# First attention: two heads stacked on the partitions, three score products of 64 rows

## The chip, the cores and the metric

The kernel runs on one core of one Trainium2 chip. The metric is the device time of one execution in microseconds (us), lower is better; times compared are medians of several runs. The engines are TensorE (PE; its weight loads are listed as PEld), VectorE (DVE), ScalarE (ACT), GpSimd (POOL) and SyncE (SP). Each has its own queue of instructions, and they meet at semaphores only.

## The reference, cut to what matters

Two layers of cross-attention and mixture of experts over x (4 x 1024 tokens of 256), with a context of 4 x 77 rows of 192. The change is in the first attention. Its queries come from x, its keys and values from the context rows and from x itself (1101 keys a batch), with 4 heads of 64:

```python
x = x + _L0_xattn_ref(ctx_768, _layernorm(x, axis=-1), mask_BxS2_bk0, ...)
...
q = ln @ Wq.T
kv = jnp.concatenate([xn @ Wkv.T, ln @ Wlkv.T], axis=1)
...
qn = rmsnorm(q, qn_g) * SCALE
kn = rmsnorm(k, kn_g)
attn = jnp.einsum('bhid,bhjd->bhij', qn, kn)
...
attn = jax.nn.softmax(attn, axis=-1)
out = jnp.einsum('bhij,bhjd->bhid', attn, v)
```

After it come the first experts stage, a second attention over the context alone, and the second experts stage.

## The kernel before, in words

The program is one sequence of stages, each a block in which every engine has its own hand-written order; a block ends when all engines are done. `attention0_inputs` (lines 115 to 302) makes the context's normalised keys `kn`, 77 rows of 16 (batch, head) pairs. `attention0` (line 332 on) runs over 4 batches of 1024 tokens, eight tiles of 128 (`TB`) each.

A number in fp32 is split into a high and a low fp16 part, h and l. Query and key are written as q = qh + ql, k = kh + kl. In `hl` each head has three pieces side by side, h, l, h again (ACT writes pieces 0 and 2 in one copy, line 608, DVE the difference into piece 1, line 723). PE turns them (lines 486 and 489): one transpose puts a head's (h, l) of 2 x 64 on 128 partitions. The queries take 4 transposes a tile, the keys 8: "form" 0 as (h, l), form 1 as (l, h). A score is then two matmuls over 128 rows: form 0 gives kh.qh + kl.ql, form 1 gives kl.qh + kh.ql.

**Tile part.** `pipeline` staggers the stages of eight tiles (`LAG` 4). Tile by tile: DVE centres (696), PE turns (462), ACT scales (591), PE projects q, k and v (473, 475), ACT squares and copies v (600, 601), DVE sums (702, 705), POOL takes the power -0.5 (674), DVE normalises (712, 716), ACT and DVE split (608, 723), PE turns the parts (486, 489), ACT copies the keys (613) and DVE the queries (727) out of PSUM. `turn_parts` of a tile waits until both copies of the tile before are done. Of every second tile, ACT and DVE also split a piece of the experts' weights (619, 752), which SP loads and stores. The first two tiles' transposes and projections of the next batch are issued at the end of the batch before.

**Loop.** 36 steps a batch (`STEPS`): 4 units (half of the queries, pair of heads) of 9 key tiles, the ninth being the 77 context rows (`kctx`). PE's order for every even n is: scores of n+1, scores of n+2, values of n, values of n+1. Scores of a step are 4 matmuls of 512 query columns (line 507), two for each of the pair's two heads; head j goes to its own PSUM bank `sc[:, n % 2, j]`. ACT makes exp of both heads in one instruction (647), DVE adds it up for the denominators (667, 663), and PE multiplies it with v in fp32, the two heads side by side on 64 columns each (518). An fp32 matmul shows as two records. Scores of step n+1 wait for the exp of step n-1 (they share banks); exp of step n waits for the sum of step n-4 (4 buffers `probs`). Behind each unit come the denominators (527), DVE's reciprocal and product (732, 736), and behind each half the output projection (540) with DVE's residual (744). ACT and DVE split one more weight piece in every unit.

POOL begins each batch with two small copies (683, 684) behind the first projection, and counts them in `vc_done`, for which PE and ACT wait before they use the context rows:

```python
pool.wait_ge(mm_done, b * TB + 1)
pool.tensor_copy(cshift[:], g.shift[0:M, bass.ds(b, 1)]).then_inc(vc_done, 1)
pool.tensor_copy(v[0:M, TB, :], g.vctx[:, bass.ds(b, 1), :].rearrange("p o d -> p (o d)")).then_inc(vc_done, 1)
```

Of the kernel before, what the change touches and what calls it, by code (L numbers as in the profile page):

```python
# [17 lines left out]
F16 = mybir.dt.float16  # L18
# [7 lines left out]
P = 128  # L26
# [86 lines left out]
def attention0_inputs(nc, g, a):  # L113


    with ExitStack() as st:
# [15 lines left out]
        khl = m.sb("khl_c", [M, B * H0, 3, HD0], F16)  # L132
# [33 lines left out]
        def _(act):  # L166
# [3 lines left out]
            for v, dst in ((a["ln_x_g"], gx), (a["ln_x_b"], bx)):  # L170
# [21 lines left out]
            act.copy(khl[:, :, 0:3:2, :], kn[:].rearrange("p (h o) d -> p h o d", o=1).to_broadcast([M, B * H0, 2, HD0])  # L192
                     ).then_inc(hi_done, 1)
            act.wait_ge(kt_done, 1)
            t16 = tr[:].bitcast(F16)
            for n in range(4):
                act.copy(g.kctx[:, n // 2, (n % 2) * 8:(n % 2) * 8 + 8, 0:M],
                         t16[:, n, 0:8 * MP].rearrange("p (h m) -> p h m", h=8)[:, :, 0:M]).then_inc(kt_ev, 1)
            act.wait_ge(kt_ev, 4)
# [22 lines left out]
        def _(dve):  # L222
# [48 lines left out]
            dve.tensor_tensor(khl[:, :, 1, :], kn[:], khl[:, :, 0, :], ALU.subtract).then_inc(v_step, 1)  # L271
# [3 lines left out]
        def _(pe):  # L275
# [22 lines left out]
            for n in range(2):  # L298
                for h in range(B * H0):
                    last = pe.transpose(t16[:, 2 * n + h // 8, (h % 8) * MP:(h % 8) * MP + M],  # L300
                                        khl[:, h, n:n + 2, :].rearrange("p o d -> p (o d)"), g.ident16[0:M, 0:M])
# [30 lines left out]
def attention0(nc, g, a):  # L332
# [7 lines left out]
    with ExitStack() as st:  # L340
# [8 lines left out]
        hl = m.sb("hl0", [P, 2, 2 * H0, 3, HD0], F16)  # L349
        qT = m.sb("qT", [P, H0, S], F16)  # L350
        kT = m.sb("kT", [P, 2, H0, S], F16)
# [15 lines left out]
        t3 = hi[:].bitcast(F16).rearrange("p a (h t) -> p a h t", t=P)  # L367
# [86 lines left out]
        def _(pe):  # L454
# [23 lines left out]
            def turn_parts(first, l):  # L478
# [6 lines left out]
                for h in range(H0):  # L485
                    pe.transpose(t3[:, 0, h, :], hl[:, i, h, 0:2, :].rearrange("p o d -> p (o d)"), g.ident16[:])
                for form in range(2):
                    for h in range(H0):
                        last = pe.transpose(t3[:, 1, form * H0 + h, :],
                                            hl[:, i, H0 + h, form:form + 2, :].rearrange("p o d -> p (o d)"), g.ident16[:])  # L490
                last.then_inc(t3_done, 1)

            def scores(b, n, fresh):
                u, k = divmod(n, KT)
                half, pair = divmod(u, 2)
                if not fresh:
                    pe.wait_ge(e_done, STEPS * b + n - 1)
                for j in range(2):
                    h = 2 * pair + j
                    q = qT[:, h, half * HALF:(half + 1) * HALF]  # L500
                    for form in range(2):
                        if k < TB:
                            kk = kT[:, form, h, k * P:(k + 1) * P]
                        else:
                            kk = g.kctx[:, form, bass.ds(b * H0 + h, 1), 0:M]
                            kk = kk.rearrange("p o m -> p (o m)")
                        last = pe.matmul(sc[0:rows(k), n % 2, j, :], kk, q, start=(form == 0), stop=(form == 1))  # L507
                last.then_inc(s_done, 1)
# [35 lines left out]
            def body(b, more):  # L544
# [6 lines left out]
                pe.wait_ge(vc_done, 2 * b + 2)  # L551
# [31 lines left out]
        def _(act):  # L583
# [19 lines left out]
            def high(first, l):  # L603
                t, i = first + l, l % 2
                act.wait_ge(n_done, t + 1)
                if l >= 2:
                    act.wait_ge(t3_done, t - 1)
                act.copy(hl[:, i, :, 0:3:2, :],
                         qk[:, i].rearrange("p (h o) d -> p h o d", o=1).to_broadcast([P, 2 * H0, 2, HD0])).then_inc(hi_done, 1)

            def keys_out(first, l):
                act.wait_ge(t3_done, first + l + 1)
                act.copy(kT[:, :, :, l * P:(l + 1) * P], t3[:, 1].rearrange("p (f h) t -> p f h t", f=2)  # L613
                         ).then_inc(e3_act, 1)
# [12 lines left out]
            def body(b, more):  # L627
# [4 lines left out]
                for n in range(STEPS):  # L632
# [11 lines left out]
                    if n == TB:  # L644
                        act.wait_ge(vc_done, 2 * b + 2)
# [1257 lines left out]
```

## Time and profile before

| | us |
|---|---|
| median of 3 runs | 1844.99 |
| lowest and highest | 1844.53, 1845.87 |
| the profiled execution | 1844.98 |
| its span in the profile | 1843.3 |
| mean granted TensorE clock | 0.922 of full |
| PE busy | 1593.0 (86%) |
| DVE, ACT, POOL busy | 1115.1, 853.1, 705.1 |
| first attention: tile part and loop of batch 1 | 58.6 to 93.2, 93.2 to 170.0 |
| of batch 4 | 445.3 to 481.1, 481.1 to 558.4 |

The span is what the profiler covers; the execution's own time is 1.7 us longer. "Idle <- releaser" in a row is how long the engine had nothing to do ahead of it, and whose instruction ended that. PE's matmul records overlap: a record lasts until its result is out, so what a matmul costs in a stream is the distance from its start to the next one's. Shapes stand as rows*columns of the weights, then the moving operand.

### The profile page before, as it was taken

What the parts mean: (1) busy time and instruction counts of PE and PEld (TensorE: products, weight loads), DVE (VectorE), ACT (ScalarE), POOL (GpSimd) and SP (SyncE); (2) the same over time, 40 slices, a digit from 0 to 9 for tenths busy, and PEclk for the clock granted to TensorE, in tenths of its full rate; (3) what the DMA queues carried; (4) which work ended last, traced back from release to release, by engine and by line L of the source; (5) the groups of instructions that cost most, each with busy time, mean ns of one, the idle gap of its engine ahead of it and who ended that gap; (6) DMA issues with size and microseconds to landing.
All of it is one profiled execution on the core that took longest, in us unless ns stands there. A gap on an engine that the chain in (4) does not pass through costs nothing. (4 is left out here: it accounts for less than half of the span.)

```text
span 1843.3 us, 38924 instructions
## 1 busy us (share of the span) xinstructions
PE 1593.0 (86%) x12460; PEld 1169.2 (63%) x12461; DVE 1115.1 (60%) x1945; ACT 853.1 (46%) x1518; POOL 705.1 (38%) x517
## 2 busy tenths in 40 slices
PE   4799798898897669999999996799988689999997
PEld 1433434434336658888888883577767568888886
DVE  4677687677687844555554441788876834444443
ACT  1664764755653425555554441376664322222221
POOL 2400401202200015555555442477771046555564
PEclk9999899899896589999999997699996789999999
DMA  4321311320414554555553222300005353333333
GB/s 132 100 79 46 114 55 36 114 68 23 138 35 168 187 206 92 137 137 137 137 137 69 46 41 38 92 25 17 8 24 180 106 149 59 59 62 60 57 60 44
DMA packets 104311, 159.85 MB, mean 87 GB/s; under 512 B 10810, under 2 KB 69998, under 8 KB 104110
## 3 DMA queue, kind: packets, MB, share of 16 engines
q1 hardware_dynamic: 73007, 117.52, 19.6%
q0 software_dynamic: 29952, 40.91, 12.6%
q8 instruction: 43, 0.70, 0.2%
q10 hardware_dynamic: 1279, 0.46, 0.1%
q14 instruction: 30, 0.25, 0.0%
HBM read 91.49 MB, written 67.37 MB: 86 GB/s over the span
## 5 line engine op out<-in xcount | busy, mean ns | idle before, releaser
L1249 PE MATMUL e_ph<-e_zTt,weights_a 128*128 128x256 f16 x3744 | 425.4, 274 | 29.3 <-issue 27.2
L1249 PEld LDWEIGHTS e_ph<-e_zTt,weights_a 128*128 x3744 | 360.9, 98 | 93.5 <-issue 49.8
L1203 POOL DMA_INDIRECT e_zt<-token_parts,slot_token x156 | 163.6, 1049 | 209.2 <-issue 198.4
L1382 DVE TENSOR_TENSOR e_hl<-e_h,e_hh 128x512 f16<-128x512 f32 x156 | 104.5, 691 | 228.4 <-ACT e_hh L1348 228.4
L1334 ACT ACTIVATE e_h<-e_ph,e_b 128x256 f32<-128x256 f32 x312 | 130.6, 470 | 232.8 <-PE e_ph L1249 155.8
L1213 POOL DMA_INDIRECT token_rows<-e_ysb,slot_token x78 | 148.2, 1901 | 206.9 <-DVE e_ysb L1399 192.5
L1263 PE MATMUL e_pyt<-weights_b,e_hh 128*128 x1248 | 210.7, 273 | 0.7 <-DVE e_ysb L1399 0.7
L647 ACT ACTIVATE probs<-lower_banks,shift 128x1024 f32<-128x1024 f32 x128 | 137.6, 1110 | 119.4 <-PE lower_banks L507 114.4
L1213 POOL DMA_INDIRECT out_dram<-e_ysb,slot_token x78 | 124.4, 1595 | 131.4 <-DVE e_ysb L1403 107.8
L1263 PE MATMUL e_pyt<-weights_b,e_hl 128*128 x624 | 170.2, 273 | 0.0
L1373 DVE SCALAR_TENSOR_TENSOR e_g<-e_ph,e_h 128x512 f32<-128x512 f32 x78 | 54.0, 692 | 174.1 <-PE e_ph L1249 174.1
L667 DVE TENSOR_TENSOR acc<-acc,probs 128x1024 f32<-128x1024 f32 (+1 forms) x112 | 136.9, 1222 | 28.7 <-ACT probs L647 25.5
L518 PE MATMUL middle_banks<-probs,v 128*64 128x512 f32 (+1 forms) x576 | 142.6, 606 | 1.0 <-ACT probs L647 1.0
L507 PE MATMUL lower_banks<-qT,kT 128*128 128x512 f16 x512 | 131.6, 402 | 4.6 <-ACT kT L613 4.6
L1263 PEld LDWEIGHTS e_pyt<-weights_b,e_hh 128*128 128x128 f16 x1248 | 122.1, 98 | 14.7 <-issue 1.0
L1337 ACT ACTIVATE e_h<-e_ph 128x512 f32<-128x512 f32 x78 | 46.6, 597 | 169.6 <-PE e_ph L1249 169.6
L507 PEld LDWEIGHTS lower_banks<-qT,kT 128*128 128x128 f16 x512 | 46.8, 101 | 106.0 <-issue 33.1
L1263 PE MATMUL e_pyt<-weights,e_hh 128*128 x624 | 108.6, 273 | 0.5 <-DVE e_ysb L1403 0.5
L683 POOL COPY cshift<-shift 77x1 f32 x4 | 0.7, 183 | 279.5 <-PE middle_banks L475 279.5
L1715 POOL TENSOR_TENSOR s<-s,rs 128x1232 f32<-128x1232 f32 x32 | 72.7, 2273 | 51.7 <-DVE rs L1783 51.6
L1348 ACT CAST e_hh<-e_h 128x512 f16<-128x512 f32 x156 | 92.3, 619 | 0.0
L1348 ACT CAST e_hh<-e_g 128x512 f16<-128x512 f32 x78 | 48.2, 618 | 83.5 <-DVE e_g L1373 83.5
(231 smaller groups left out, 2952.5 us busy)
## 6 DMA issues: line engine op xcount, KB each, us to landing
weight_parts<-w_split SPq DMA_DIRECT2D x32, 512.0 KB, 3.3
weights_a<-weight_parts SPq DMA_DIRECT2D x16, 1024.0 KB, 7.4
x_sb<-in_u SPq DMA_DIRECT2D x24, 512.0 KB, 5.1
weight_parts<-x_sb SPq DMA_DIRECT2D x24, 512.0 KB, 3.4
w_raw<-in_w1T SPq DMA_DIRECT2D x16, 512.0 KB, 4.4
w_raw<-in_w2T SPq DMA_DIRECT2D x16, 512.0 KB, 4.7
weights_b<-weight_parts SPq DMA_DIRECT2D x8, 1024.0 KB, 9.6
token_parts<-x_sb SPq DMA_DIRECT2D x8, 1024.0 KB, 5.3
```

The source lines that it names most:

```text
L507: last = pe.matmul(sc[0:rows(k), n % 2, j, :], kk, q, start=(form == 0), stop=(form == 1))
L518: last = pe.matmul(po[u % 2][j * HD0:(j + 1) * HD0, :], v[0:rows(k), k, h * HD0:(h + 1) * HD0], pr[0:rows(k), n % 4, j, :], start=(k == 0) ...
L647: act.activation(pr[0:r, n % 4], sc[0:r, n % 2], ACT.Exp, bias=bias).then_inc(e_done, 1)
L667: dve.tensor_tensor(acc[0:r, u % 2], acc[0:r, u % 2], pr[0:r, n % 4], ALU.add).then_inc(acc_done, 1)
L1203: pool.indirect_dma_start(zt[:, i % 2, c, :], None, g.zrows, at).then_inc(ld[i % 2], 16)
L1213: pool.indirect_dma_start(g.rows[layer], at, ysb[:, s, c, :], None, compute_op=ALU.add).then_inc(sto[s], 16)
L1249: last = pe.matmul(ph[:, q, f, :], up_w(wp, e, k, 2 * q + f), zTs[:, s, 2 * zp + k, :], start=(n == 0), stop=(n == 5))
L1263: last = pe.matmul(py[c][:, 0, :], hp[:, s, f, c * P:(c + 1) * P], down_w(wp, e, f), start=(n == 0), stop=(n == 3 * NF - 1))
L1334: last = act.activation(h32[:, q % 2, f, :], ph[:, q, f, :], ACT.Relu, bias=b1[:, bass.ds(e, 1), 2 * q + f], scale=1.0 / WS)
L1348: act.copy(hh[:, s, 2 * q:2 * q + 2, :], src[:, q % 2]).then_inc(hi_done, 1)
L1382: dve.tensor_tensor(hl[:, s, 2 * q:2 * q + 2, :], src[:, q % 2], hh[:, s, 2 * q:2 * q + 2, :], ALU.subtract).then_inc(lo_done, 1)
L1715: pool.tensor_tensor(s[:, i], s[:, i], per_key(rs[:, i, :]), ALU.mult).then_inc(n_done, 1)
```

## The change

Query and key parts are now laid out as high parts of all heads, then low parts of all heads (`hl[:, i, part, head]`), with no third piece. One transpose takes the same part of two neighbouring heads, so that the pair's heads stand on partitions 0 to 63 and 64 to 127; a tile takes 4 transposes for the queries and 4 for the keys. `qT` and `kT` have the indices part and pair. A score is three products of 64 rows: kh.qh, kh.ql, kl.qh (kl.ql is left out), and the six matmuls of a step go head 0, head 1, head 0, head 1 and so on. The context keys are laid out in the same way (16 transposes instead of 32, two copies instead of four), and POOL copies a batch's context keys behind its 1024 keys in `kT`, so that all steps read `kT`; `vc_done` counts three a batch.

```diff
@@ -129,7 +129,7 @@
         kn = m.sb("kn_c", [M, B * H0, HD0])
-        khl = m.sb("khl_c", [M, B * H0, 3, HD0], F16)
+        khl = m.sb("khl_c", [M, 2, B * H0, HD0], F16)
         mask = m.sb("mask_c", [M, B], U8)
@@ -189,14 +189,13 @@
             act.wait_ge(v_step, 16)
-            act.copy(khl[:, :, 0:3:2, :], kn[:].rearrange("p (h o) d -> p h o d", o=1).to_broadcast([M, B * H0, 2, HD0])
-                     ).then_inc(hi_done, 1)
+            act.copy(khl[:, 0], kn[:]).then_inc(hi_done, 1)
             act.wait_ge(kt_done, 1)
             t16 = tr[:].bitcast(F16)
-            for n in range(4):
-                act.copy(g.kctx[:, n // 2, (n % 2) * 8:(n % 2) * 8 + 8, 0:M],
-                         t16[:, n, 0:8 * MP].rearrange("p (h m) -> p h m", h=8)[:, :, 0:M]).then_inc(kt_ev, 1)
-            act.wait_ge(kt_ev, 4)
+            for n in range(2):
+                act.copy(g.kctx[:, n, :, 0:M],
+                         t16[:, n, 0:2 * B * MP].rearrange("p (h m) -> p h m", m=MP)[:, :, 0:M]).then_inc(kt_ev, 1)
+            act.wait_ge(kt_ev, 2)
 
@@ -268,7 +267,7 @@
             dve.wait_ge(hi_done, 1)
-            dve.tensor_tensor(khl[:, :, 1, :], kn[:], khl[:, :, 0, :], ALU.subtract).then_inc(v_step, 1)
+            dve.tensor_tensor(khl[:, 1], kn[:], khl[:, 0], ALU.subtract).then_inc(v_step, 1)
             dve.wait_ge(v_step, 22)
@@ -296,9 +295,9 @@
             for n in range(2):
-                for h in range(B * H0):
-                    last = pe.transpose(t16[:, 2 * n + h // 8, (h % 8) * MP:(h % 8) * MP + M],
-                                        khl[:, h, n:n + 2, :].rearrange("p o d -> p (o d)"), g.ident16[0:M, 0:M])
+                for h in range(2 * B):
+                    last = pe.transpose(t16[:, n, h * MP:h * MP + M],
+                                        khl[:, n, 2 * h:2 * h + 2, :].rearrange("p o d -> p (o d)"), g.ident16[0:M, 0:M])
             last.then_inc(kt_done, 1)
@@ -346,9 +345,9 @@
         qk = m.sb("qk0", [P, 2, 2 * H0, HD0])
-        hl = m.sb("hl0", [P, 2, 2 * H0, 3, HD0], F16)
-        qT = m.sb("qT", [P, H0, S], F16)
-        kT = m.sb("kT", [P, 2, H0, S], F16)
+        hl = m.sb("hl0", [P, 2, 2, 2 * H0, HD0], F16)
+        qT = m.sb("qT", [P, 2, 2, S], F16)
+        kT = m.sb("kT", [P, 2, 2, S + MP], F16)
         v = m.sb("v0", [P, KT, D])
@@ -364,7 +363,7 @@
         pv = [mid[:, i, 0:D] for i in range(2)]
-        t3 = hi[:].bitcast(F16).rearrange("p a (h t) -> p a h t", t=P)
+        t3 = hi[:].bitcast(F16).rearrange("p a (h t) -> p a h t", t=P)[:, :, 0:4, :].rearrange("p a (f n) t -> p a f n t", f=2)
         sc = lo[:].rearrange("p (s j) q -> p s j q", s=2)
@@ -482,12 +481,12 @@
                     pe.wait_ge(e3_dve, t)
-                for h in range(H0):
-                    pe.transpose(t3[:, 0, h, :], hl[:, i, h, 0:2, :].rearrange("p o d -> p (o d)"), g.ident16[:])
-                for form in range(2):
-                    for h in range(H0):
-                        last = pe.transpose(t3[:, 1, form * H0 + h, :],
-                                            hl[:, i, H0 + h, form:form + 2, :].rearrange("p o d -> p (o d)"), g.ident16[:])
+                for what in range(2):
+                    for part in range(2):
+                        for pair in range(2):
+                            h = what * H0 + 2 * pair
+                            last = pe.transpose(t3[:, what, part, pair, :],
+                                                hl[:, i, part, h:h + 2, :].rearrange("p o d -> p (o d)"), g.ident16[:])
                 last.then_inc(t3_done, 1)
@@ -495,16 +494,12 @@
                     pe.wait_ge(e_done, STEPS * b + n - 1)
-                for j in range(2):
-                    h = 2 * pair + j
-                    q = qT[:, h, half * HALF:(half + 1) * HALF]
-                    for form in range(2):
-                        if k < TB:
-                            kk = kT[:, form, h, k * P:(k + 1) * P]
-                        else:
-                            kk = g.kctx[:, form, bass.ds(b * H0 + h, 1), 0:M]
-                            kk = kk.rearrange("p o m -> p (o m)")
-                        last = pe.matmul(sc[0:rows(k), n % 2, j, :], kk, q, start=(form == 0), stop=(form == 1))
+                for product, (kp, qp) in enumerate(((0, 0), (0, 1), (1, 0))):
+                    for j in range(2):
+                        dims = slice(j * HD0, (j + 1) * HD0)
+                        last = pe.matmul(sc[0:rows(k), n % 2, j, :], kT[dims, kp, pair, k * P:k * P + rows(k)],
+                                         qT[dims, qp, pair, half * HALF:(half + 1) * HALF],
+                                         start=(product == 0), stop=(product == 2))
                 last.then_inc(s_done, 1)
@@ -548,7 +543,7 @@
                 pe.wait_ge(e3_dve, first + TB)
-                pe.wait_ge(vc_done, 2 * b + 2)
+                pe.wait_ge(vc_done, 3 * b + 3)
                 scores(b, 0, True)
@@ -605,13 +600,11 @@
                     act.wait_ge(t3_done, t - 1)
-                act.copy(hl[:, i, :, 0:3:2, :],
-                         qk[:, i].rearrange("p (h o) d -> p h o d", o=1).to_broadcast([P, 2 * H0, 2, HD0])).then_inc(hi_done, 1)
+                act.copy(hl[:, i, 0], qk[:, i]).then_inc(hi_done, 1)
 
 ...
                 act.wait_ge(t3_done, first + l + 1)
-                act.copy(kT[:, :, :, l * P:(l + 1) * P], t3[:, 1].rearrange("p (f h) t -> p f h t", f=2)
-                         ).then_inc(e3_act, 1)
+                act.copy(kT[:, :, :, l * P:(l + 1) * P], t3[:, 1]).then_inc(e3_act, 1)
 
@@ -642,7 +635,7 @@
                     if n == TB:
-                        act.wait_ge(vc_done, 2 * b + 2)
+                        act.wait_ge(vc_done, 3 * b + 3)
                     bias = g.shift[:, B:B + 1] if k < TB else cshift[:]
@@ -681,6 +674,7 @@
                 pool.tensor_copy(cshift[:], g.shift[0:M, bass.ds(b, 1)]).then_inc(vc_done, 1)
+                pool.tensor_copy(kT[:, :, :, S:S + M], g.kctx[:, :, bass.ds(2 * b, 2), 0:M]).then_inc(vc_done, 1)
                 pool.tensor_copy(v[0:M, TB, :], g.vctx[:, bass.ds(b, 1), :].rearrange("p o d -> p (o d)")).then_inc(vc_done, 1)
@@ -720,11 +714,11 @@
                 dve.wait_ge(hi_done, t + 1)
-                dve.tensor_tensor(hl[:, i, :, 1, :], qk[:, i], hl[:, i, :, 0, :], ALU.subtract).then_inc(lo_done, 1)
+                dve.tensor_tensor(hl[:, i, 1], qk[:, i], hl[:, i, 0], ALU.subtract).then_inc(lo_done, 1)
 
 ...
                 dve.wait_ge(t3_done, first + l + 1)
-                dve.tensor_copy(qT[:, :, l * P:(l + 1) * P], t3[:, 0, 0:H0, :]).then_inc(e3_dve, 1)
+                dve.tensor_copy(qT[:, :, :, l * P:(l + 1) * P], t3[:, 0]).then_inc(e3_dve, 1)
 
@@ -1846,7 +1840,7 @@
             m = Mem(nc, st)
-            g.kctx = m.sb("kctx", [P, 2, B * H0, MP], F16)
+            g.kctx = m.sb("kctx", [P, 2, 2 * B, MP], F16)
             g.vctx = m.sb("vctx", [M, B, D])
```

## Rows read from the trace of the kernel before

**Rows 1.** Busy time by stretch (93.2:170.0, 221.7:299.1, 351.6:429.0, 481.1:558.4), the four loops

```profile
core 0: us, PE busy (x) PEld busy (x) DVE busy (x) ACT busy (x) POOL busy (x), PEclk, DMA share, GB/s
...
sum 308.90, PE 303.69 PEld 102.69 DVE 234.14 ACT 171.82 POOL 4.17; mean PE 75.92 PEld 25.67 DVE 58.54 ACT 42.95 POOL 1.04
```

**Rows 2.** The same view, the four tile parts (58.6, 187.0, 315.6, 445.3 on)

```profile
sum 141.10, PE 103.99 PEld 66.96 DVE 107.34 ACT 108.13 POOL 67.15; mean PE 26.00 PEld 16.74 DVE 26.83 ACT 27.03 POOL 16.79
```

**Rows 3.** The page, part 2: granted TensorE clock in 40 slices of 46 us

```profile
PEclk9999899899896589999999997699996789999999
```

**Rows 4.** Timeline, second batch's loop: start, us, engine line op out<-in xcount [idle <-releaser]

```profile
248.16 1.90 PE L507 MATMUL lower_banks<-qT,kT 128*128 128x512 f16 x8
249.33 1.11 ACT L647 ACTIVATE probs<-lower_banks,shift 128x1024 f32<-128x1024 f32 x1 [2.46 <-PE lower_banks L507]
249.99 1.94 PE L518 MATMUL middle_banks<-probs,v 128*64 128x512 f32 x8
250.35 1.05 ACT L619 ACTIVATE w_split<-w_raw 128x1024 f16<-128x1024 f32 x1
...
251.29 1.10 ACT L647 ACTIVATE probs<-lower_banks,shift 128x1024 f32<-128x1024 f32 x1
...
251.86 1.90 PE L507 MATMUL lower_banks<-qT,kT 128*128 128x512 f16 x8
```

**Rows 5.** Groups of the page: line engine op out<-in xcount | busy us, mean ns | idle

```profile
L507 PE MATMUL lower_banks<-qT,kT 128*128 128x512 f16 x512 | 131.6, 402 | 4.6 <-ACT kT L613 4.6
```

**Rows 6.** Timeline of PE, one tile of the second attention, and a projection of the first

```profile
1206.66 0.81 PE L1652 MATMUL psc<-kcur,qT 32*128 32x154 f32 x16
...
208.43 1.03 PE L475 MATMUL middle_banks<-wqkv,lnT 128*128 128x256 f32 x4
```

**Rows 7.** Timeline, half 0's output and the end of the second batch's loop

```profile
276.29 0.69 DVE L744 TENSOR_TENSOR x_sb<-x_sb,upper_banks 128x512 f32 x1 [1.05 <-PE upper_banks L540]
277.03 1.99 PE L540 MATMUL upper_banks<-wo,oT 128*128 128x256 f32 x8 [0.96 <-DVE x_sb L744]
...
287.49 3.36 DVE L732 RECIPROCAL rden<-upper_banks 128x512 f32<-128x512 f32 x1 [0.18 <-PE upper_banks L527]
...
291.49 4.99 DVE L667 TENSOR_TENSOR acc<-acc,probs 128x1024 f32<-128x1024 f32 x4
...
297.53 2.47 DVE L667 TENSOR_TENSOR acc<-acc,probs 128x1024 f32<-128x1024 f32 x2
...
300.38 0.44 PE L462 MATMUL lower_banks<-ident,z 128*128 128x128 f32 x2 [1.34 <-DVE z L696]
```

**Rows 8.** Timeline, two tiles of the second batch's tile part

```profile
197.67 1.03 ACT L613 COPY kT<-upper_banks 128x1024 f16<-128x1024 f16 x1
...
199.68 1.23 DVE L752 SCALAR_TENSOR_TENSOR w_split<-w_raw,w_split 128x1024 f16<-128x1024 f32 x1 [0.48 <-ACT w_split L619]
```

**Rows 9.** Groups of the page, an ACT cast of 512 elements in the experts stage

```profile
L1348 ACT CAST e_hh<-e_h 128x512 f16<-128x512 f32 x156 | 92.3, 619 | 0.0
```

**Rows 10.** Timeline, end of the second tile part and the first scores

```profile
209.52 0.61 PE L489 MATMUL upper_banks<-ident,hl 128*128 128x128 f16 x8
...
219.48 1.06 PE L489 MATMUL upper_banks<-ident,hl 128*128 128x128 f16 x8
220.58 1.01 ACT L613 COPY kT<-upper_banks 128x1024 f16<-128x1024 f16 x1 [1.85 <-PE upper_banks L489]
...
221.72 5.28 PE L507 MATMUL lower_banks<-qT,kT 128*128 128x512 f16 x12 [1.18 <-ACT kT L613]
```

**Rows 11.** Timeline, the context stage

```profile
38.17 6.50 POOL L329 TENSOR_TENSOR rstd<-stat_ve,neghalf 128x32 f32<-128x32 f32 x1 [3.58 <-DVE stat_ve L323]
...
39.25 1.90 ACT L192 CAST khl_c<-kn_c 77x2048 f16<-77x2048 f32 x1 [8.19 <-DVE kn_c L254]
...
42.55 2.24 PE L300 MATMUL tr_c<-ident,khl_c 77*128 77x77 f16 x32 [13.44 <-DVE khl_c L271]
...
44.82 2.40 ACT L197 COPY kctx<-tr_c 128x616 f16<-128x616 f16 x4 [3.67 <-PE tr_c L300]
```

**Rows 12.** Groups of the page, POOL's first copy of a batch

```profile
L683 POOL COPY cshift<-shift 77x1 f32 x4 | 0.7, 183 | 279.5 <-PE middle_banks L475 279.5
```

## The prediction

> **What bounds the kernel now.** I read the 40 slices first, then the busy time by stage, the waits and groups of TensorE (PE), and last the timeline of one stage. The change touches the first attention and the short context stage ahead of it alone, so the question is what sets the pace there. The rest follows it in a chain and should move as a whole.
>
> The first attention has four batches, each with two parts. In the **loop** (36 steps: scores, exp, values) PE is busy 303.7 us of 308.9, VectorE (DVE) 234, ScalarE (ACT) 172 [rows 1]. So PE sets the pace, with DVE at 76%. In the **tile part** (eight tiles: projection, norm, split, transposes; 141.1 us in the four) PE is busy 104, DVE 107, ACT 108, about three quarters each [rows 2]. There no engine is the bound: they wait for one another in turn. The PEclk line is at 9 tenths in this stretch (slices 2 to 12), but at 8 in the fifth, eighth and eleventh, where a tile part ends [rows 3]: PE runs at its lower level, 1.2 GHz, for a while there.
>
> Inside the loop, a pair of steps is eight score matmuls, then eight value records. The scores start at 248.16 and last 1.90 us, the values start at 249.99, the next scores at 251.86 [rows 4]: a period of 3.70 us for two steps. Eight score matmuls in 1.90 us, the last taking 0.38 from its start, are one per (1.90 - 0.38) / 7 = 0.217 us, near enough to the 0.213 of 512 columns at 2.4 GHz. The score group is 512 such matmuls, 131.6 us busy [rows 5], and 64 more over the context keys.
>
> **Scores, three products for four.** Before: 4 matmuls of 128 rows a step. After: 6 of 64 rows, alternately on partitions 0-63 and 64-127, into different banks. What six cost hangs on whether the two halves of the array run side by side. The trace has no 64-row pair, but it has a 32-row group: L1652 puts 16 records of 154 columns, four row groups in turn, into 0.81 us [rows 6]. Their neighbour of 256 columns runs 4 records in 1.03 us, (1.03 - 0.38) / 3 = 0.215 each [rows 6], so 154 columns should take 0.13, and 16 in series 2.1 us. They took 0.81: row groups do run side by side. Bounds for one pair of matmuls: 0.217 us (perfect overlap) to 0.434 (none). I take 0.217, as the 32-row row is much nearer to overlap. A step is then 3 x 0.217 = 0.65 instead of 0.87, a gain of 0.217 (with exact streaming, 0.214) a step, 7.7 us a batch, **30.9 us** over 144 steps, if nothing else ends last.
>
> The Trainium skill, page "TensorE: Matmul & The Clock Gate", section "Measured speedup vs the span model", gives 3.07x for four row tiles of 512 columns, and also a model in which tiles cost some 4 ns each. By the model the gain is the 30.9; by 3.07 of 4, applied to two, a pair would cost 1.3 matmuls and three pairs nearly as much as four matmuls do now. The rows settle less than I would like; this is a rival below.
>
> **What takes some of it back in the loop.**
> - ACT's extra weight cast of 1.05 us, once in 9 steps, sits between two exps (249.33 and 251.29), and the second ends at 252.39 [rows 4]. The second half of the scores from 251.86 waits for it; it starts at 252.72 now. After the change it would want to start 0.64 earlier (three pair slots saved), at 252.08, while the exps are only 0.21 earlier, at 252.18: 0.1 to 0.2 us with the semaphore, four times a batch: 0.8 at most.
> - For an ordinary pair of steps: the first exp starts 1.17 us after its scores and could start 0.21 earlier, so it ends 1.17 - 0.21 + 1.11 = 2.07 after the scores begin. The values that need it are the second half of the group from 249.99, some 0.9 behind that time: 2.7 after the scores begin, then 2.3 [rows 4]. The slack shrinks from 0.4 to 0.2: no stall.
> - DVE in 9 steps: 8 sums of 1.25 (four take 4.99), 4.00 from the reciprocal's start to the next sum, one weight split of 1.25: 15.3 us [rows 7, 8]. PE's nine steps are 9 x 1.85 and about 0.9 for the denominators (half a value group), 17.5, and become 15.6. It fits on average, not locally. After the reciprocal at 287.49, DVE runs without a break through 291.49 + 4.99 and the last sums at 297.53 + 2.47 = 300.0, and PE's first transpose of the next batch waits 1.34 us for it at 300.38 [rows 7]. So the batch's last 12.5 us are DVE's already: the 5 steps of scores that PE does behind 287.49 give nothing, 5 x 0.214 = 1.07 us lost a batch.
> - The output of the first half waits 0.96 us between its two halves for DVE's residual, which now starts as soon as PE is done (DVE idle 1.05 before it) [rows 7]. PE arrives 1.3 us earlier, DVE does not: I put 0.7 us a batch on it.
>
> Loop in all: 7.7 - 0.8 - 1.1 - 0.7 = 5.1 a batch, **20.6 us**. Bounds: 30.9 (all hidden) and about 12 (twice these losses and more at the start of a unit).
>
> **Tile part.** ACT's split copy and key copy go from 1024 written elements to 512: 1.03 us for the key copy now [rows 8], 0.62 for an ACT cast of 512 elsewhere [rows 9], so about -0.42 each. DVE's subtraction and query copy keep their 512 elements. Transposes go from 12 to 8: 8 in 0.61 at full and 1.06 at half clock, so 0.056 or 0.107 each [rows 8, 10], -0.22 or -0.43.
> - Middle: in a tile with a weight piece DVE waits 0.48 for ACT's weight cast, which is behind the key copy [rows 8]. That goes; then comes DVE's own order, norm to sums to POOL's power to norm, which the change leaves. Two such tiles a batch: -1.0.
> - Tail: the last tiles wait on one another. The last transposes end at 220.54, the key copy follows, the scores start at 221.72 after it [rows 10]. Fewer transposes -0.43, key copy -0.43, and the weight cast behind the previous key copy, which holds up DVE, moves by both, of which I count 0.75: -1.6.
> Together -2.6 a batch, **-10.2 us**; bounds 0 below (if DVE and POOL alone set the pace) and 16 above.
>
> The first 12 score matmuls of a batch take 5.28 us, 0.427 each: half clock [rows 10]. Three slots of it cost 1.3 less, but the clock then comes back later in the work; I count them at 0.214 like the rest, and leave ±1 us a batch.
>
> **Context stage.** The chain: cast of 2048 elements 1.90 us, 32 transposes 2.24, four copies 2.40, ending 47.22; POOL's power ends at 44.67 [rows 11]. After: cast about 1.0 (half the elements), 16 transposes -1.0, two copies -1.2, together -3.1; but POOL's 44.67 becomes the last. **-2.5 us**; bounds 0 to 3.1.
>
> **POOL's new copy** of context keys (308 elements) joins two copies, the first of 0.18 us, which start after 279.5 us of idle time in four goes [rows 12]; behind it is only the power of the next tile. It is hidden under the projection and squares; without that cover, under 1 us a batch. PE and ACT wait for one more vc_done, long in. SP's queue is not touched.
>
> **Sum.** 20.6 + 10.2 + 2.5 = 33.3 off. The profiled run took 1844.98 us (span 1843.3), the median is 1844.99, so no correction: **1811.7 us**.
>
> **Rivals.**
> 1. Row groups overlap poorly. L1652's 16 records are four rounds, three gaps in 0.81 - 0.29 = 0.52, 0.17 each, where 154 columns need 0.13: 1.3 times. If that isn't just the first round after a switch, three pairs cost 3 x 0.28 = 0.85, as now. Only the 12.7 outside the loop stays: 1832. For: the arithmetic. Against: the scores' own first gap behind the values is hardly longer than the others (eight in 1.90 us leave no room for it) [rows 4], and that a first round is long after a change of layout explains the rest. Chance 0.1. The skill's 3.07x (same page) would give the same 1832.
> 2. DVE becomes the bound of the whole loop. Then units run at 15.3 plus gaps in DVE from waits for exp, and the loop gains 10 to 12: 1844.98 - 12.7 - 11 = 1821. For: no-idle DVE in the last unit. Against: 234 of 309 busy. The skill's "TensorEngine Tiling (Array Packing)", section "PSUM Bottleneck", says just this: a faster array leaves the evacuation as it was. Chance 0.15.
> 3. **Slower**: the two 64-row groups don't overlap with 128 weight columns each, so six matmuls take 6 x 0.214. Place: the score line; price 2 x 0.214 x 144 = 61.8, less 12.7: +49, 1894. It decides as soon as a pair costs over 1.5 matmuls. Against: L1652 has 128 weight columns too, in fp32, and overlaps [rows 6]. Chance 0.08.
> 4. All hidden, clock returns early: -30.9 - 12.7 - 2: 1799. Chance 0.12.
>
> **Chances.** Forecast 0.55, rivals as above. The range 1798 to 1828 takes in the forecast, rivals 2 and 4 and the bounds of the loop's losses; it leaves out 1 and 3 and the forecast's own tails. A measurement here can tell about 0.2% (3.7 us) from no change. Faster by more 0.89; within 0.03, the worst of rival 1, where the tile part gives nothing either; slower 0.08, rival 3.
>
> **What would show it.** The score line: 864 records, starting in pairs a few ns apart, pairs 0.214 apart; busy some 100 to 110 us, with the context keys' (before, 131.6 for the 512 alone). If single records stand 0.214 apart, rival 3. The loop near 72 us a batch instead of 77.2 (308.9 / 4), with more waits of PE for exp and DVE; if DVE is over 90% busy there, rival 2. The tile part near 32.7 us a batch from 35.3 (141.1 / 4), with the DVE wait on the weight cast gone. The key and split copies at 0.6 us. The first z at 45.2. If the copies are short and the tile part as long as before, POOL and DVE were its bound and step "tile part" is wrong.

## Result, and the profile after

The changed kernel takes 1812.56 us (median of 4 runs, 1811.81 to 1814.75), the kernel before 1845.24 (4 runs): a ratio of 0.9825, 95% interval [0.9808, 0.9842], or 32.7 us less. Forecast were 1811.7 us, 33.5 less than the 1845.2 measured here, and a range of 1798 to 1828. The number came out within 1 us; not all parts of the sum did.

The two profiled executions, 1843.3 and 1810.7 us in span, cut at the same points of the work:

| stretch | before | after | difference | forecast |
|---|---|---|---|---|
| context stage, up to the first z | 47.7 | 44.9 | -2.8 | -2.5 |
| tile parts, from the first split copy to the first scores | 141.1 | 128.9 | -12.2 | -10.2 |
| loops, from the first scores to the last values | 308.9 | 278.9 | -30.0 | -30.9, less 10.3 |
| from a loop's last values to the next tile part, or to the stage's end | 63.7 | 71.3 | +7.6 | part of the 10.3 |
| everything behind the first attention | | | +4.8 | 0 |

The groups of the changed kernel's page, which answer to [rows 5] and [rows 12] (line engine op out<-in xcount | busy us, mean ns | idle before):

```profile
L500 PE MATMUL lower_banks<-qT,kT 64*128 64x512 f16 (+1 forms) x864 | 114.5, 397 | 2.9 <-ACT kT L607 2.9
...
L676 POOL COPY cshift<-shift 77x1 f32 x4 | 0.7, 183 | 255.7 <-PE middle_banks L474 255.7
```

864 records are busy 114.5 us, somewhat more than the 100 to 110 forecast; of the kernel before, the 512 over x's keys alone were busy 131.6. The loops take 69.7 us a batch (278.9 / 4), where about 72 was forecast: part of the loss that I had put into the loop came behind it.

Busy time by stretch, changed kernel: the four loops, the four tile parts, then the four stretches behind the loops (columns as in [rows 1]):

```profile
core 0: us, PE busy (x) PEld busy (x) DVE busy (x) ACT busy (x) POOL busy (x), PEclk, DMA share, GB/s
...
sum 278.90, PE 272.12 PEld 86.42 DVE 229.24 ACT 171.67 POOL 4.17; mean PE 68.03 PEld 21.61 DVE 57.31 ACT 42.92 POOL 1.04
...
sum 128.90, PE 92.56 PEld 56.52 DVE 104.00 ACT 81.78 POOL 67.28; mean PE 23.14 PEld 14.13 DVE 26.00 ACT 20.45 POOL 16.82
...
sum 71.30, PE 47.77 PEld 27.96 DVE 45.30 ACT 12.14 POOL 9.84; mean PE 11.94 PEld 6.99 DVE 11.32 ACT 3.04 POOL 2.46
```

PE is still busy 98% of the loops; DVE has come up from 76% to 82%. The timeline of a unit (start, us, what) answers to [rows 4]:

```profile
232.45 1.47 PE L500 MATMUL lower_banks<-qT,kT 64*128 64x512 f16 x12
233.41 1.11 ACT L640 ACTIVATE probs<-lower_banks,shift 128x1024 f32<-128x1024 f32 x1 [2.02 <-PE lower_banks L500]
233.85 1.94 PE L513 MATMUL middle_banks<-probs,v 128*64 128x512 f32 x8
234.42 1.05 ACT L612 ACTIVATE w_split<-w_raw 128x1024 f16<-128x1024 f32 x1
...
235.37 1.10 ACT L640 ACTIVATE probs<-lower_banks,shift 128x1024 f32<-128x1024 f32 x1
...
235.72 1.63 PE L500 MATMUL lower_banks<-qT,kT 64*128 64x512 f16 x12
```

Twelve matmuls in 1.47 us where eight took 1.90: six slots instead of eight. The period of two steps is 3.27 us (232.45 to 235.72) instead of 3.70. The second group takes 1.63, 0.16 more: that is the wait for the exp behind ACT's weight cast, forecast at 0.1 to 0.2. In each batch two pairs of steps are longer in this way, by 0.06 to 0.16, not four.

Behind the loop, changed kernel, the same places as [rows 7]:

```profile
258.84 1.99 PE L535 MATMUL upper_banks<-wo,oT 128*128 128x256 f32 x8 [1.33 <-DVE x_sb L738]
...
268.43 3.36 DVE L726 RECIPROCAL rden<-upper_banks 128x512 f32<-128x512 f32 x1
...
278.47 2.47 DVE L660 TENSOR_TENSOR acc<-acc,probs 128x1024 f32<-128x1024 f32 x2
...
281.32 0.44 PE L461 MATMUL lower_banks<-ident,z 128*128 128x128 f32 x2 [2.25 <-DVE z L690]
```

From the reciprocal to the last sum's end DVE needs 12.5 us as before (268.43 to 280.94, then 287.49 to 300.00). PE gets through its last scores faster and waits 2.25 us for z instead of 1.34; the output waits 1.33 instead of 0.96.

The tile part (answers to [rows 8] and [rows 10]):

```profile
187.85 0.60 ACT L607 COPY kT<-upper_banks 128x512 f16<-128x512 f16 x1
...
189.44 1.23 DVE L746 SCALAR_TENSOR_TENSOR w_split<-w_raw,w_split 128x1024 f16<-128x1024 f32 x1 [0.15 <-ACT w_split L612]
...
205.17 1.01 PE L488 MATMUL upper_banks<-ident,hl 128*128 128x128 f16 x8 [2.31 <-DVE qT L721]
...
207.24 1.01 PE L488 MATMUL upper_banks<-ident,hl 128*128 128x128 f16 x8 [1.06 <-DVE qT L721]
208.28 0.59 ACT L607 COPY kT<-upper_banks 128x512 f16<-128x512 f16 x1 [1.48 <-PE upper_banks L488]
...
209.00 4.13 PE L500 MATMUL lower_banks<-qT,kT 64*128 64x512 f16 x18 [0.75 <-ACT kT L607]
```

The key copy is 0.60 instead of 1.03, DVE's wait for the weight cast 0.15 instead of 0.48, and the last groups of transposes follow each other 2.07 us apart (205.17 to 207.24) instead of 2.86 (216.62 to 219.48). The scores start at half clock as before, 18 of them in 4.13 us.

### The profile page after: what moved, and what is told of

Its sections match the earlier page's. It is cut to its first block and busy times, and to the rows that moved or that the text cites. A ratio compares the mean times of both kernels' runs of the same rounds, so it can differ in the third digit from the quotient of the medians.

```text
span 1810.7 us, 39194 instructions
## 1 busy us (share of the span) xinstructions
PE 1554.4 (86%) x12604; PEld 1143.3 (63%) x12605; DVE 1110.4 (61%) x1945; ACT 824.6 (46%) x1516; POOL 706.7 (39%) x521
## 5 line engine op out<-in xcount | busy, mean ns | idle before, releaser
L500 PE MATMUL lower_banks<-qT,kT 64*128 64x512 f16 (+1 forms) x864 | 114.5, 397 | 2.9 <-ACT kT L607 2.9
L500 PEld LDWEIGHTS lower_banks<-qT,kT 64*128 64x128 f16 (+1 forms) x864 | 37.4, 99 | 99.9 <-ACT probs L640 41.9
L1612 PE MATMUL pt<-ident,s 128*77 128x128 f32 x512 | 73.8, 290 | 14.6 <-ACT pT L1675 7.0
```

Source lines behind the costliest of these rows:

```text
L500: last = pe.matmul(sc[0:rows(k), n % 2, j, :], kT[dims, kp, pair, k * P:k * P + rows(k)], qT[dims, qp, pair, half * HALF:(half + 1) * HALF ...
L1612: last = pe.transpose(pt[:, n % 2, h % 4, :], s[:, d % SLOT, h, :], g.ident[:])
```

## Experiments

Each kernel ran with the kernel before on the same chip; times are medians of 4 runs, and single runs for the two second traces. The kernel before gave 1846.2 in the first two groups of runs and 1847.1 in the third.

**The order of the six matmuls.**

```diff
-                for product, (kp, qp) in enumerate(((0, 0), (0, 1), (1, 0))):
-                    for j in range(2):
+                for j in range(2):
+                    for product, (kp, qp) in enumerate(((0, 0), (0, 1), (1, 0))):
```

> The changed kernel with the same six 64-row matmuls a step, but head 0's three first, then head 1's three. Theory A (neighbours in different row groups run side by side, and that is the whole gain of the loop): now only head 0's last runs beside head 1's first, and across two steps head 1's last beside head 0's first; 9 slots of 0.214 us for two steps instead of 6, so +1.5 x 0.214 x 144 = +46 us, 1859 us. Rival B (a 64-row matmul is cheaper by itself, whatever its neighbour): no change, 1812 to 1814 us.

Measured: 1815.2 us (0.9835 of before, [0.9819, 0.9852]), 2.6 more than the changed kernel, whose own runs spread over 2.9. Neither 1859 nor a clean proof of B. The timeline of PE:

```profile
243.53 1.48 PE L500 MATMUL lower_banks<-qT,kT 64*128 64x512 f16 x12
```

Twelve in 1.48 us as in turns. In the records the starts still come in pairs, some 9 ns apart where the changed kernel has 3. The records don't name the partitions, so which two ran side by side is an inference: if matmuls on the same rows can't overlap (the next run), head 1's first, queued fourth, ran beside head 0's first. PE then doesn't need neighbours of different row groups, and the part "in turns" of the change does nothing that can be told here. Whether the pair ran abreast at all needed a kernel that can't do it:

**All six on one row group.**

```diff
-                        dims = slice(j * HD0, (j + 1) * HD0)
+                        dims = slice(0, HD0)
```

> The changed kernel with all six matmuls of a step on partitions 0 to 63 (the second head's scores are made from the first head's data; the work is the same in number and size). e1_no_turns has shown that the order of the six does not matter. Theory A (two row groups run side by side, in whatever order they are queued): here nothing can, six slots instead of three, +3 x 0.214 x 144 = +92, less what the slower loop gives back by DVE being on time, about 8: 1897 us. Theory B (a 64-row matmul is cheaper by itself): 1813 us.

Head 1's scores are then made of head 0's data, so this kernel's output is not the attention's; it serves for the time alone. Measured: 1910.7 us, ratio 1.0338 [1.0321, 1.0356]; 98 us above the changed kernel. Timeline of PE, the four loops, and the four stretches behind them:

```profile
261.82 2.32 PE L500 MATMUL lower_banks<-qT,kT 64*128 64x512 f16 x10
...
265.94 2.76 PE L500 MATMUL lower_banks<-qT,kT 64*128 64x512 f16 x12
```

```profile
sum 386.70, PE 381.88 PEld 131.90 DVE 237.90 ACT 177.89 POOL 4.17; mean PE 95.47 PEld 32.97 DVE 59.48 ACT 44.47 POOL 1.04
```

```profile
sum 61.50, PE 43.13 PEld 27.00 DVE 38.50 ACT 12.24 POOL 9.84; mean PE 10.78 PEld 6.75 DVE 9.62 ACT 3.06 POOL 2.46
```

Twelve take 2.76 us, (2.76 - 0.38) / 11 = 0.216 each: a 64-row matmul costs as much as one of 128 rows, and the whole gain of the loop is two row groups side by side. Theory B is out. This is also what rival 3 would have cost: 1911, not the prediction's 1894, nor the 1897 expected here. DVE's slack did come back: the stretches behind the loops are 61.5 us, 9.8 less than in the changed kernel, where I had credited 8. What was too low is the price of the loops, 107.8 us more instead of 92. An ordinary pair of steps takes 4.56 us against 3.27, which makes 93 of it over the 72 pairs of the four batches; the rest lies at the loops' half-rate starts (the first 18 score matmuls of the second batch last 7.86 us against 4.13). The stages behind the attention took 3.3 us more as well.

**A fourth product, and only two.**

```diff
-                for product, (kp, qp) in enumerate(((0, 0), (0, 1), (1, 0))):
+                for product, (kp, qp) in enumerate(((0, 0), (0, 1), (1, 0), (1, 1))):
...
-                                         start=(product == 0), stop=(product == 2))
+                                         start=(product == 0), stop=(product == 3))
```

> The changed kernel with the fourth product kl.ql put back: eight 64-row matmuls a step in turns. It keeps the new layout, transposes and copies. Theory A: four slots a step, the loop is as long as in the kernel before, and only what the tile part and the context stage gave is left: +6.3 us a batch, about 1838 us; each product is worth a slot of 0.214 us, less what DVE took back. Rival B (the gain of the loop came from elsewhere, as from the fewer weight columns read or the copies): 1813 to 1820 us.

> The changed kernel with kh.ql left out as well: two products, four matmuls, two slots a step. If PE still sets the loop alone, it gains another 0.214 x 144 = 30.9 us: 1782 us. If DVE, with 15.3 us of work in 9 steps against 15.6 of PE's now and 13.7 then, is the next bound, the loop gains only some 2 to 3 us a batch: about 1802 us, with DVE over 85% busy in the loop. I expect the second.

Measured: 1835.8 us with four (0.9944, [0.9927, 0.996]), 1802.0 with two (0.9767, [0.9744, 0.979]). The four loops of each:

```profile
sum 307.50, PE 302.56 PEld 102.45 DVE 233.98 ACT 171.61 POOL 4.17; mean PE 75.64 PEld 25.61 DVE 58.49 ACT 42.90 POOL 1.04
```

```profile
sum 266.30, PE 247.21 PEld 68.59 DVE 225.48 ACT 170.10 POOL 5.18; mean PE 61.80 PEld 17.15 DVE 56.37 ACT 42.53 POOL 1.30
```

With four products the loops last 307.5 us, as in the kernel before (308.9). So the layout gives the loop nothing and the third slot everything: 307.5 to 278.9 is 28.6 us, 0.199 a step. The next slot gives 12.6 us, not 28.6: PE's share falls from 98 to 93%, and its longest wait in the loop is now for DVE's residual (waits of PE, second batch's loop; this wait was 1.3 us with three products):

```profile
PE upper_banks L535 <- DVE x_sb L738: 3.3, 1, 3.3
PE lower_banks L500 <- ACT probs L640: 1.0, 3, 0.4
```

DVE's lateness is the next limit that shows, and close, though DVE itself is busy 85% of these loops, not over 90. The four runs spread from 1799.6 to 1807.7 us; the time is the 1802 forecast. Whether DVE alone sets the pace of this loop wasn't tried.

The Trainium skill says that tiling makes PE faster and leaves the evacuation of PSUM as it was ("TensorEngine Tiling (Array Packing)", section "PSUM Bottleneck"). At three slots no run here shows such a limit. At two, the residual that PE waits for does read PSUM, but most of DVE's work in the loop, the sums over `probs`, reads SBUF, so these runs don't show that the evacuation is what held it up.

**The reciprocal on ACT.** This takes 3.4 us a unit away from DVE. The cut shows the main lines; ACT's call for a batch's last unit stands at the head of the next batch, or behind the last loop:

```diff
+            def invert(b, u):
+                act.wait_ge(den_done, UNITS * b + u + 1)
+                if u > 0:
+                    act.wait_ge(o_done, UNITS * b + u)
+                act.activation(rden[:], pden, ACT.Ln).then_inc(ln_done, 1)
+                act.wait_ge(ln_done, UNITS * b + u + 1)
+                act.activation(rden[:], rden[:], ACT.Exp, scale=-1.0).then_inc(r_done, 1)
...
+                    if n in (KT + 4, 2 * KT + 3, 3 * KT + 4):
+                        invert(b, n // KT - 1)
...
-                dve.wait_ge(den_done, UNITS * b + u + 1)
-                dve.reciprocal(rden[:], pden).then_inc(r_done, 1)
```

> The changed kernel with the reciprocal of the denominators (3.36 us on DVE) made on ACT as exp(-ln(x)), two instructions of about 0.6 us. Theory C (DVE's lateness at the end of a batch is what took back part of the gain: PE waits 2.25 us for the next batch's z, and the last output waits for the reciprocal): about 2.2 + 2 us a batch go, 1796 us. Rival (DVE's lateness is covered by PE's and POOL's own chain): under 4 us, 1809 to 1813 us. If the two ACT instructions hold up exp in the loop, slower by 0.5 us a unit, +8 us.

> The kernel before the change, with the reciprocal on ACT as exp(-ln(x)), as in e4_rden_on_act. Theory C (DVE's lateness took back part of the change's gain): the kernel before gains less from this, 1.3 us of waiting for z and 2 us of the last output's chain a batch, 13 us: 1832 us; the change then brings 38 to 39 us (1832 to 1793) instead of 33. Rival (the two are independent): 1845.2 - 19.4 = 1826 us.

Measured: 1793.2 us on the changed kernel (ratio to the kernel before 0.9719, [0.9703, 0.9736]), the fastest version here; on the kernel before 1832.1 (0.9923, [0.9906, 0.9939]). With both on ACT the change brings 38.9 us (1832.1 to 1793.2) instead of 32.7, the 38 to 39 of theory C; the rival's 1826 is out. The four loops of the first, and the four stretches behind them:

```profile
sum 277.90, PE 272.99 PEld 86.19 DVE 196.80 ACT 186.04 POOL 4.17; mean PE 68.25 PEld 21.55 DVE 49.20 ACT 46.51 POOL 1.04
```

```profile
157.70:172.20 14.50, 11.55 (x45) 7.29 (x46) 7.27 (x17) 5.19 (x13) 3.25 (x5) 1.00 0.16 49
...
505.00:516.00 11.00, 6.38 (x20) 4.28 (x20) 3.83 (x9) 1.23 (x2) 0.00 (x0) 0.84 0.08 29
```

The loops are as long as before (277.9), so in them DVE's 32 us less (229.2 to 196.8) change next to nothing. Most of the gain comes behind them: the four stretches take 54.2 us instead of 71.3, which is 17.1 of the 23.0 us between the two traces (19.4 between the medians); 14.5 instead of 18.7 from the last values of the first batch to the next tile part, 11.0 instead of 16.3 at the end. PE waits 0.7 us for z (2.25 in the changed kernel), and the clock stays at full rate there (PEclk 1.00 in the first row; 0.91 in the changed kernel, below). The traced execution is the fastest of its four (1789.5 us; the slowest took 1795.9), and another 4.1 us of its lead over the changed kernel's trace lie in the stages behind the attention (1271.7 instead of 1275.9). So the 38.9 isn't DVE's lateness alone: between the traces of the two kernels with the reciprocal on ACT, the change gives back under 1 us behind the loops, where it was 7.6, but also only 0.4 in the stages behind, where it was 4.8.

**The tile part.** Four more transposes a tile, then ACT's copies at 1024 elements on top:

```diff
+                for part in range(2):
+                    for pair in range(2):
+                        pe.transpose(t3x[:, 1, part, pair, :],
+                                     hl[:, i, part, 2 * pair:2 * pair + 2, :].rearrange("p o d -> p (o d)"), g.ident16[:])
```

```diff
-                act.copy(hl[:, i, 0], qk[:, i]).then_inc(hi_done, 1)
+                act.copy(hl[:, i, 0:3:2], qk[:, i].rearrange("p (o h) d -> p o h d", o=1).to_broadcast([P, 2, 2 * H0, HD0])).then_inc(hi_done, 1)
...
-                act.copy(kT[:, :, :, l * P:(l + 1) * P], t3[:, 1]).then_inc(e3_act, 1)
+                act.copy(kT8[:, :, l * P:(l + 1) * P], hi[:].bitcast(F16).rearrange("p a (h t) -> p a h t", t=P)[:, 1]).then_inc(e3_act, 1)
```

> The changed kernel with four more transposes a tile (12 as before), into PSUM columns that nothing reads. The prediction's tail has the last transposes and, through the weight cast, those of a tile before on the path, 0.43 us each at half clock; the middle tiles cost nothing, since DVE and POOL set the pace. So +0.4 to +0.9 us a batch: 1814.5 to 1816 us. Rival (PE sets the pace of the tile part): 0.22 to 0.43 us in each of 32 tiles, +9 us, 1821 us.

> As e5_twelve_turns, and ACT's two copies of a tile write 1024 elements again, as in the kernel before (the second half goes to places that nothing reads). The tile part should then be as before: by the prediction +2.6 us a batch, 10.2 in all, 1823 us, most of it from the copies. Rival (the tile part was bound by DVE and POOL, and its shortening came from the clock's phase or from the new layout of DVE's writes): under +4 us, 1816 us.

Measured: 1819.0 us with the transposes (0.9851, [0.9835, 0.9868]) and 1825.7 with both (0.9888, [0.9872, 0.9905]): +6.4 and +13.2. The four tile parts of each:

```profile
sum 132.90, PE 102.67 PEld 65.92 DVE 104.31 ACT 82.00 POOL 67.32; mean PE 25.67 PEld 16.48 DVE 26.08 ACT 20.50 POOL 16.83
```

```profile
sum 139.30, PE 101.63 PEld 66.13 DVE 107.18 ACT 108.25 POOL 67.70; mean PE 25.41 PEld 16.53 DVE 26.80 ACT 27.06 POOL 16.93
```

In the tile parts themselves the transposes cost 4.0 us (128.9 to 132.9) and the copies 6.4 more, and the sum of 10.4 is the forecast's 10.2. The 1.0 a batch for the transposes is above my 0.4 to 0.9, but part of it is the clock. A tile part of the changed kernel has two lengths: 31.8 to 32.1 us (PEclk 0.89 to 0.91), or 33.2 (0.87), the latter in the second batch of its first trace and in the third of its second. With the four transposes the batches take 32.7, 33.9, 33.8 and 32.5: 0.7 more than 32.0, 33.2 and 31.8 in the first, second and fourth, and in the third 0.6, set beside the longer kind. Like set beside like, the transposes cost 0.7 a batch, as forecast.

Neither theory's total fits, 1816 or 1821 with the transposes: 2.4 and 2.8 us of the two fell outside the tile parts, where the two kernels do the same as the changed one. In the traces, 1.9 of the first lies in the stages behind the attention; of the second, 1.1 lies ahead of the first tile part, whose start moves by 0.8 between the changed kernel's own two traces. The reason isn't shown.

**What was given back behind the attention.** The stage behind starts 37.4 us earlier (572.3 to 534.9), the end comes 32.6 earlier. The missing 4.8 us can be chance, other in each execution, or come back with the kernel. Both kernels were traced again, one execution each:

> The changed kernel as it is, for a second trace. In the first one the first attention ended 37.4 us earlier than in the kernel before, but the whole only 32.6. [...] Rival (what was given back is a cost of the change): the same 4 to 5 us are given back again, at the same places.

> The kernel before as it is, for a second trace. [...] Rival: the two traces run alike to 0.3 us everywhere.

Measured: 1814.8 and 1848.7 us. In the second pair the stage behind starts 37.6 us earlier and the end comes 33.9 earlier, so 3.7 us are given back. The stages behind took 1271.0 and 1273.1 us in the two traces of the kernel before, 1275.9 and 1276.8 in those of the changed one: a kernel differs from itself by 0.9 or 2.1 us, and from the other by 2.8 to 5.8.

Two places make up most of it. The first is 20 us of the first experts stage, at the same point of the work: the kernel before, its second trace, the changed kernel, its second trace:

```profile
690.00:710.00 20.00, 19.55 (x186) 17.24 (x187) 7.13 (x15) 10.82 (x24) 10.89 (x8) 1.00 0.33 54
```

```profile
691.60:711.60 20.00, 19.55 (x186) 17.33 (x187) 7.18 (x15) 10.76 (x24) 10.89 (x8) 1.00 0.33 54
```

```profile
652.60:672.60 20.00, 19.19 (x167) 16.20 (x168) 6.97 (x15) 9.69 (x21) 9.85 (x8) 0.91 0.28 41
```

```profile
654.30:674.30 20.00, 19.11 (x166) 16.27 (x167) 6.90 (x15) 9.62 (x21) 10.46 (x8) 0.91 0.28 41
```

The changed kernel has a piece of 1.2 GHz there, PEclk 0.91, where the kernel before has 1.00, and gets 167 matmuls done instead of 186. It is one group of 48 that takes 7.08 us instead of 5.41 (timelines of PE, the kernel before, then the changed one):

```profile
689.92 5.41 PE L1249 MATMUL e_ph<-e_zTt,weights_a 128*128 128x256 f16 x48 [1.79 <-issue]
```

```profile
653.00 7.08 PE L1243 MATMUL e_ph<-e_zTt,weights_a 128*128 128x256 f16 x48 [2.08 <-issue]
```

The second place, ahead of the second attention, is no matter of the clock, which is at half rate there in all four traces (PEclk 0.50). DVE waits longer for a load of x (timelines of DVE, the kernel before, then the changed one):

```profile
1157.19 0.43 DVE L1749 BATCH_NORM_STATS2 stats<-x_sb 128x6 f32<-128x256 f32 x1 [2.46 <-DMA x_sb<-token_rows]
```

```profile
1123.77 0.43 DVE L1743 BATCH_NORM_STATS2 stats<-x_sb 128x6 f32<-128x256 f32 x1 [4.09 <-DMA x_sb<-token_rows]
```

In the second traces it waits 2.54 and 3.92 us. PE's next work waits for the z that DVE makes of it, 9.40 us instead of 7.77. A last 1.1 us is lost at the start of the second experts stage in the first pair; in the second pair that loss is made up again.

So both large pieces came back in both traces of a kernel, which makes pure chance unlikely. They aren't a price of the new layout either: the kernel with the reciprocal on ACT has it and took 1271.7 us behind the attention in its trace, its counterpart without the change 1271.3, and the kernels with twelve transposes have it and wait 2.5 us for the load. The kernel with four products and the one on a single row group lose there too (1277.4 and 1279.2 us). It is work that the change doesn't touch. What decides where the half-rate pieces fall and how long the load takes wasn't tried and stays open.

## Why the prediction was right, point by point

- **Bound and main term: right.** PE set the loops' pace, and a pair of 64-row matmuls costs one slot (rows of the fp32 group with 32 rows carried this over [rows 6]). Forecast 30.9 us in the loops before losses; 28.6 between the kernels with four and three products. Rival 1, poor overlap, is out; so is the reading of the Trainium skill's 3.07x for four tiles as 1.5x for two ("TensorE: Matmul & The Clock Gate", "Measured speedup vs the span model"). That section's other model, a few ns for each tile, agrees: 12 records in 1.47 us, in pairs that start some 3 ns apart.
- **What is taken back: the size roughly right, the place not.** The forecast had 10.3 us, all counted in the loops. Measured are 8.5: 0.9 in the loops (30.9 less 30.0) and 7.6 in the stretches behind them. I put 1.1 us a batch on DVE's lateness at the end and 0.7 on the output. Measured in the second batch: 0.91 more waiting for z, and 0.37 more at the output, so that term was twice too large. I put up to 0.8 a batch on ACT's weight cast: it is at most 0.16 for each of two groups, 0.3. A part I hadn't listed is the clock. The stretch from the second batch's last values to the next tile part runs partly at 1.2 GHz, as the row of the changed kernel shows beside the one before:

```profile
279.10:297.20 18.10, 13.45 (x45) 7.77 (x46) 12.14 (x19) 4.07 (x11) 3.25 (x5) 0.91 0.17 58
```

```profile
299.10:315.60 16.50, 11.77 (x45) 7.28 (x46) 11.20 (x18) 4.04 (x10) 2.85 (x4) 1.00 0.18 57
```

  The same 45 matmuls are busy 13.45 us instead of 11.77, and that is the whole difference of 1.6 between the two stretches. The changed kernel has 0.91 there in all three batches that have a next one; the kernel before has 0.90 in its first batch and 1.00 in two; with the reciprocal on ACT, where PE waits only 0.7 us for z, it is 1.00 in all three. In the first batch, where both kernels ran partly at the lower level, the 1.7 us lost are idle time of PE. That the longer wait brings the clock down fits these rows; it wasn't tried by itself.
- **Tile part: right.** 12.2 us measured, 10.2 forecast; some of the 12.2 is the clock, as two tile parts of the kernel before were of a longer kind (36.0 and 35.8 us against 34.6 and 34.7) and one of the changed kernel. Like set beside like it is 2.6 to 2.8 a batch, some 11 in all. The copies cost 6.4 us when widened again and the transposes 0.7 a batch. Of DVE's wait for the weight cast 0.15 us is left, where I had written that it goes.
- **The prediction's own sums** hold to 0.2 us: 4 x 5.1 is 20.4, not 20.6, and 4 x 2.6 is 10.4, not 10.2, which cancel.
- **Context stage: right.** z starts 2.8 us earlier, 0.3 of it from a load; POOL's power, not the keys, is now the last.
- **POOL's copy: right.** It takes 0.44 us, in idle time.
- **The step that was missing** is what happens behind the attention. I wrote that the rest "should move as a whole". It gave back 4.8 us, and 3.7 in the second pair of traces. Without that the change would have brought 37.4 us where I forecast 33.3: the losses were 1.8 smaller, the tile part 2.0 and the context stage 0.3 larger. That the total came out within 1 us is luck, a gain forecast too low against a loss that I hadn't seen.
- **Rival 2** (DVE bounds the loop): not at three products, since taking 32 us from DVE left the loops at 277.9. At two products PE waits for DVE, but DVE is busy 85%, below the 90 that I had named as the sign.
- **Rival 3** (no overlap) was priced too low: forced, it gives 1911 us, not 1894.

## What to carry to other kernels

A contraction over 64 rows that is stacked up to 128 to fill the array can be taken apart again: two matmuls on different halves of the partitions, into different banks, cost one slot here (12 in 1.47 us), so three products of two heads cost three slots, not four. Before taking more from the bound engine, look at who finishes last at the end of a loop: here a 3.36 us reciprocal on DVE was worth 19 us on the changed kernel and 14 on the one before, with next to no effect inside the loop (1.0 us). And split an expected gain at the stage's end as well as at the kernel's: in stages that weren't touched, one group of matmuls met a half-rate piece of the clock (1.7 us) and one load took longer (1.6 us).

## What was not expected of the hardware

- The order of matmuls on two row groups didn't matter: three for rows 0 to 63 queued ahead of three for rows 64 to 127 took 1.48 us for two steps, against 1.47 in turns. By strict order of the queue, nine slots would have been needed for two steps, and a slot of one row group costs 0.216; so matmuls of different row groups don't start in the order of the queue. The records don't say which of them ran side by side.
- The stages behind the attention are the same work in all these kernels, and took from 1271.0 to 1279.2 us in their traces, while a second trace of the same kernel differed by 0.9 and 2.1 us.
- A fourth product as a fourth pair gave the old loop to within 1.4 us of 308.9, so going back and forth between 64-row and 64-column layouts costs no more than between 128 rows and 64 columns.
- exp(-ln(x)) on ACT, 0.60 and 0.63 us for 512 columns, replaced a DVE reciprocal of 3.36 us.
